# Widening a block's rows on ScalarE instead of VectorE, and scaling the routed rows ahead of the gelu

## What is computed

```python
logits = xt @ Wr + br
probs = softmax(logits)
top_p, top_idx = top_k(probs, 2)
weights = top_p / top_p.sum(axis=-1, keepdims=True)
xn = (xt - mu) * rsqrt(var + LN_EPS)
xe = xn[None, :, :] * ln_g[:, None, :] + ln_b[:, None, :]
h = gelu(einsum('end,edh->enh', xe, W1) + b1[:, None, :], approximate=False)
y = einsum('enh,ehd->end', h, W2) + b2[:, None, :]
out = (weights[:, :, None] * sel).sum(axis=1)
```

## Time and profile before

| | us |
|---|---|
| median of 3 runs | 3103.79 |
| lowest and highest | 3102.59, 3106.05 |
| the profiled execution | 3109.04 |
| its span in the trace | 3107.2 |
| blocks begin, about | 2237 into the span |
| blocks with tiles, two a step | about 2320 to 2771 |
| blocks alone | about 2771 to 3098 |

### The profile page before, as it was taken

The page is one execution under the profiler, slowest core; times in us unless marked ns, Lnnn a source line. Parts: engine busy times, 40 slices in busy tenths (PEclk is TensorE's granted clock), DMA queues, the critical chain, the costliest instruction groups (busy, mean ns, idle before and its releaser), DMA issues. The chain is left out here.

```text
span 3107.2 us, 76649 instructions
## 1 busy us (share of the span) xinstructions
PE 2657.0 (86%) x21213; PEld 1906.9 (61%) x21213; DVE 1716.7 (55%) x6061; ACT 1507.1 (49%) x4666; POOL 1972.3 (63%) x2053
## 2 busy tenths in 40 slices
PE   8898878878788878878888787885589999999998
PEld 6665445545454544545444444553479999999998
DVE  6466555555555555555555555556676556553222
ACT  5555444444444444444444454443466566554332
POOL 7277777777777777777777777775455455343222
PEclk9999988889898889888889898887599999999999
DMA  7688888888888888888888888886667677667664
GB/s 232 190 236 249 238 248 238 245 242 240 247 240 247 239 242 245 239 249 239 243 245 241 246 238 244 241 239 188 206 209 216 200 225 217 191 192 208 188 182 127
DMA packets 292076, 701.47 MB, mean 226 GB/s; under 512 B 44041, under 2 KB 139680, under 8 KB 291797
## 3 DMA queue, kind: packets, MB, share of 16 engines
q0 software_dynamic: 151888, 456.15, 52.2%
q1 hardware_dynamic: 140036, 243.55, 25.5%
HBM read 633.18 MB, written 66.36 MB: 225 GB/s over the span
## 5 line engine op out<-in xcount | busy, mean ns | idle before, releaser
L257 POOL DMA_INDIRECT e_kv<-d_kv,idx x1566 | 1498.6, 957 | 532.2 <-issue 510.5
L500 PE MATMUL psK<-consts,e_kv 128*128 128x128 f32 x3132 | 555.3, 305 | 295.9 <-DMA e_kv<-d_kv,idx 291.5
L500 PEld LDWEIGHTS psK<-consts,e_kv 128*128 128x128 f32 x3132 | 373.3, 152 | 430.0 <-issue 418.9
L397 DVE COPY e_kT<-psK 128x384 f32<-128x384 f32 x522 | 289.7, 555 | 323.9 <-PE psK L500 320.8
L1591 POOL DMA_INDIRECT out<-f_y,f_whose x105 | 166.9, 1590 | 473.2 <-DMA out<-f_y,f_whose 241.9
L1659 ACT ACTIVATE f_hT<-f_psH,f_b 128x128 f32<-128x128 f32 x840 | 237.0, 372 | 352.9 <-PE f_psH L2114 347.9
L2114 PE MATMUL f_psH<-f_xT,f_w 128*128 128x128 f32 x3360 | 400.1, 278 | 0.9 <-DVE f_xT L1957 0.9
L2114 PEld LDWEIGHTS f_psH<-f_xT,f_w 128*128 128x128 f32 x3360 | 391.7, 194 | 3.5 <-issue 1.3
L2127 PE MATMUL f_psY<-f_w,f_hT 128*128 x1680 | 381.8, 380 | 6.0 <-DVE f_yb L1967 4.1
L336 ACT COPY e_kT<-psK 128x384 f32<-128x384 f32 x522 | 249.9, 479 | 244.7 <-PE psK L500 227.3
L330 ACT COPY e_qb<-QT 64x32 f32 x1044 | 229.3, 220 | 279.2 <-issue 251.5
(11 more groups left out here) (309 smaller groups left out, 4013.3 us busy)
## 6 DMA issues: line engine op xcount, KB each, us to landing
f_w<-in_W SPq DMA_DIRECT2D x113, 1024.0 KB, 5.2
e_rows<-d_feat SPq DMA_DIRECT2D x174, 288.0 KB
e_kv<-d_kv,idx POOLq DMA_INDIRECT x1566
d_accs<-e_accs SPq DMA_DIRECT2D x87, 195.0 KB
f_xs<-d_xs SPq DMA_DIRECT2D x105, 132.5 KB, 4.9
d_kv<-p_kv SPq DMA_DIRECT2D x48, 256.0 KB, 2.1
p_x<-in_x SPq DMA_DIRECT2D x49, 128.0 KB, 2.9
n_v<-d_kv SPq DMA_DIRECT2D x49, 128.0 KB, 4.9
```

The lines of the kernel that those rows point to most:

```text
L257: pool.indirect_dma_start(out=kv[g.slot][:, t, :], out_offset=None, in_=kv_dram[:, :], in_offset=bass.IndirectOffsetOnAxis(ap=idx[g.slot][ ...
L397: dve.tensor_copy(kT[a.slot % 2][:, 0, j * GH:(j + 1) * GH], psK[:, 0, 0:GH]).then_inc(s_kTv, 1)
L500: mm = pe.transpose(psK[:, half, t * P:(t + 1) * P], kv[a.slot][:, third * TS + t, half * P:(half + 1) * P], ident)
```

## The change

`widen` leaves VectorE. ScalarE gets a function `widened`, laid at the head of a step for its first block, and for the second block behind the first one's gelu. It reads the expert's number into a register, and `bent` uses that same register, where it read its own before. Each of the two instructions is an activation of the function Identity, whose scale and bias are the expert's columns of `f_ln`. `sent` moves in steps with blocks from behind the first block's gelu to ahead of it.

```diff
-            def bent(g):
+            def widened(g):
                 if g == 0:
                     act.wait_ge(s_cv, 3)
+                act.wait_ge(s_T, g + 1)
+                e = act.value_load(rows[0:1, g:g + 1], min_val=0, max_val=NX - 1)
+                if g >= 2:
+                    act.wait_ge(s_h, (g - 1) * FC)
+                for a in range(DC):
+                    act.activation(xT[g % 2][:, a, :], psT[:, a * BK:(a + 1) * BK], ACT.Identity,
+                                   bias=ln[:, a, bass.ds(e + NX, 1)], scale=ln[:, a, bass.ds(e, 1)]).then_inc(s_xT, 1)
+                return e
+
+            def bent(g, e):
                 table(ACT.Gelu)
-                act.wait_ge(s_h, g * FC + FB)
-                e = act.value_load(rows[0:1, g:g + 1], min_val=0, max_val=NX - 1)
                 for f in range(FC):
...
                 if k is not None and not here:
                     gate(k)
+                expert = [widened(g) for g in here[0:1]]
                 if b is not None or k is not None:
                     table(ACT.Sqrt)
...
                 if not here:
                     sent(s)
+                if here:
+                    sent(s)
                 for u, g in enumerate(here):
-                    bent(g)
-                    if u == 0:
-                        if k is not None:
-                            gate(k)
-                        sent(s)
+                    if u:
+                        expert.append(widened(g))
+                    bent(g, expert[u])
+                    if u == 0 and k is not None:
+                        gate(k)
...
-            def widen(g):
-                dve.wait_ge(s_T, g + 1)
-                e = dve.value_load(rows[0:1, g:g + 1], min_val=0, max_val=NX - 1)
-                if g >= 2:
-                    dve.wait_ge(s_h, (g - 1) * FC)
-                for a in range(DC):
-                    dve.tensor_scalar(xT[g % 2][:, a, :], psT[:, a * BK:(a + 1) * BK],
-                                      ln[:, a, bass.ds(e, 1)], ln[:, a, bass.ds(e + NX, 1)],
-                                      ALU.mult, ALU.add).then_inc(s_xT, 1)
...
                 if here:
                     for _ in first:
                         pass
-                    widen(here[0])
...
-                    for g in here[1:]:
-                        widen(g)
```

## The result

The changed kernel takes 3128.24 us (median of 4 runs, 3127.48 to 3131.43), the kernel before 3104.53 in the same comparison. The ratio is 1.0075, 95% interval 1.0063 to 1.0086: slower by 24 us, where 32 were forecast.

The account below looks back on a forecast made before the run. PE's list was taken to bound the kernel, with ScalarE's `n_h` ending last in 21 steps. Terms +29.8 + 5 + 1.6 - 4 = +32, laid on the median 3103.79, gave 3136 us, range 3112 to 3153.

Parts of the forecast that it names:

- What bounds it: From 2320 on PE's list sets the time; in 21 two-block steps ScalarE's piece from last gelu to `n_h` ends last.
- Widening ahead of `n_h`: At the head of two-block steps, `n_h` 1.15 us later, 21 steps paying it in full; +29.8 us together.
- The pair: The widening's two Identity activations on ScalarE, put at 0.86 us, bounded by 0.64 and 1.08.
- the register load: ScalarE's read of the expert's number between last gelu and table load, taken as 0.39 us, bounds 0 and 0.82.
- rival B: Same mechanism, smaller: load hidden under the gelus, pair near 0.64, routed rows free; +11, 3115 us; chance 24%.
- Gelus 0.1 us earlier: Gelus of the block before no longer wait for a register load of their own; 0.1 us gained at most.
- Second block and blocks alone: There PE's second product covers the widening, with 1.0 us of cover; cost nothing.
- Routed rows: Laid ahead of the first block's gelu, they delay it in 8 steps with three tiles; +5 us (0 to 10).
- First block: Its widening, needing the transposes, stands before `n_h`, so the first product starts later, once; +1.6 us.
- VectorE relieved: Each block frees 1.12 us on VectorE, which shortens steps of one block and later waits around GpSimd; -4 us.
- Table loads and the other lists: Table loads keep number and kind, and PE's, GpSimd's and SP's lists stay the same; nothing.
- Rival C: Faster: VectorE makes steps long, so taking 1.12 us per block from it counts; 3091 us; chance 9%.

Follow-up runs that it names:

- k4_before_nh_first: The kernel before with `n_h` ahead of `n_xn` in steps with blocks, nothing else; 3100.38 us, ratio 0.9990.
- k1_sent_back: The changed kernel with the scaling of the routed rows put back behind the first block's gelu; 3120.34 us, ratio 1.0054 to the kernel before.
- k10_second_only: The kernel before with only the second block of each step widened on ScalarE; ratio 1.0004, on a slower chip.
- k3_nh_first: The changed kernel with routed rows put back and step heads ordered `n_h`, widening, `n_xn`; 3095.20 us, ratio 0.9976 to the kernel before.
- k7_again: The changed kernel with superfluous widening work at VectorE's old places, second run, on a slower chip; ratio 1.0055 to the kernel before.

## Why the prediction was right, and where it was off

- **What bounds it.** Right. PE's list sets the pace, and in 21 steps `n_h` already ended last; `k4_before_nh_first` took exactly the 0.31 us of the earlier trace rows off a plain step. The constant 0.73 us between `n_h` and PE's transposes holds in every kernel where `n_h` is the last to come.
- **Widening ahead of `n_h`, +29.8.** Mechanism right, size too large. Forecast 1.15 us per step, measured 0.75 in a plain step, in 27 steps 20 us. Measured in one piece, from the `n_h` of step 23 to that of step 50, `k1_sent_back` took 17.3 us more than the kernel before (467.1 against 449.8), in which the 2.4 us of waits for VectorE are already given back. The pair was near: 0.81 for 0.86; that it is 0.08 slower than VectorE's 0.73 is worth 2 us of the 20. The term that failed is the register load, taken as 0.39 from the earlier trace rows. On ScalarE it costs 0: its sequencer begins to read at 2328.92, when two of the gelus (2329.04 and 2329.29) have yet to begin. VectorE's sequencer, in the earlier trace rows, begins only after the predecessor has:

```profile
L1953 DVEq TENSOR_LOAD <-rows x1: 313/313/313, 2386.5 to 2386.5; - x1
```

The predecessor starts at 2386.52 and runs 0.42 us; from the load's start to the widening's it is 0.8. My explanation of the difference: the gelus don't wait for one another, so the sequencer hands them on and goes ahead; in VectorE's chain each operation waits for the one before, and the sequencer with it. Shown are the two starts, the hidden first load and the 0.55 us of the second; no run changed the predecessor alone. The prediction had both bounds and chose the wrong one, and with it rival B's argument was the better one on this point: with the load at 0 its own sum would have been +22, near the 24 measured.
- **Gelus 0.1 us earlier, -0.1 per step.** Nothing came of it. They start earlier, but in two groups of four, and the second still waits for the end of the first product, 0.64 us in the row above.
- **Second block and blocks alone, 0.** Right: `k10_second_only`'s plain step is 16.55, and PE is busy 318.1 of 319 us in the last window.
- **Routed rows, +5 (0 to 10).** Right in kind and within its range, toward the upper end: 6.5 us by the times, 7.1 and 10.2 by the stage. The raw sum of 10.5 was reduced for waits given back. PE waited 8.2 for `f_hT`, and 2.4 of waits for `f_yb` and `f_y` vanished.
- **First block, +1.6.** The first product starts 118.4 us into the stage instead of 116.3: +2.1 in this pair of traces, +1.3 in that of `k1_sent_back`.
- **VectorE relieved, -4.** The sum is about right by luck, the place wrong. From the first product to step 23, where it was forecast, only 1.0 us came back; PE still waited 3.45 us for `n_h` where it had waited 4.21, and the product behind that pause was still slow, 6.38 us, at a granted clock of 0.66 from 2280 to 2290. Behind step 50, where nothing was forecast, 3.0 came back.
- **Table loads and the other lists, 0.** Nothing in the traces speaks against it.
- **Rival C and the rule of balance.** VectorE at 272 of 451 us was not what PE waited for, so relieving it moved a few microseconds. The Trainium skill (Perfetto Trace Analysis, Optimizing Scalar/DVE Operations) suggests such a move where VectorE is saturated. This VectorE wasn't, and the trace agrees so far as the move brought little; no run here has a saturated one.

The signs came as forecast, each somewhat smaller: from the last gelu's end to `n_h` 2.75 us (3.2 was forecast), PE's wait there 0.87 (1.4), and the mean of the 23 steps 17.8 ((2741.68 - 2332.42) / 23; 18.0). The forecast of +32 was off by 8: the load was put too high by 10.5, the routed rows too low by a few.

The stage grew by 25.6 us: 20 (`n_h`) + 7 (routed rows, less the waits given back) + 2.1 (first block) - 1.0 - 3.0 = 25. How the 27.5 us of the 27 steps divide depends on the side from which one comes: taken out of the changed kernel the routed rows are 10.2 of them and leave 17.3 for the widening; added to the kernel before they are 6.0 and leave 21.5.

## What to carry to other kernels

Before work is moved to the less busy engine, look at what stands behind the place in its list into which it goes: two activations in front of the one on which PE waits cost 20 us, and the same two behind it nothing. That `k3_nh_first` is even faster than the kernel before comes in good part from `n_h` having passed `n_xn` too, which `k4_before_nh_first` does with no work moved at all. A pause of a tenth of a microsecond that the profile calls "issue" may be a dependence; a distance that is the same in every step tells. In these traces a register load was free behind gelus, with 0.75 us of them left to run, cost 0.55 us as a second load behind the first, and left a hole of 0.39 us behind a chain in which each operation waits for the one before.

## What the runs showed that was not expected

ScalarE hides one register load under the last gelus, and charges 0.55 us for the second. Swapping two neighbours in ScalarE's list, `n_xn` and `n_h`, and moving no work, makes the kernel before faster by 3.7 us (7.2 in the stage).

The two chips of the last eight runs took 3811 and 3802 us for the kernel before, 700 more than the first ones. The trace of `k7_again` on one of them and that of the kernel before move the same bytes, 701.5 MB; the mean rate is 183 against 226 GB/s because the span is longer:

```profile
DMA packets 292078, 701.50 MB, mean 183 GB/s; under 512 B 44040, under 2 KB 139679, under 8 KB 291796
```

The stage starts 2751.6 us into the span instead of 2123.3, so most of the 700 lies ahead of what was changed. Within it, steps in which batches are scattered take 21 to 26 us instead of the changed kernel's 18 to 19, while plain steps agree to 0.01 us with those of the first chips: 17.30 for the widening as changed, 16.24 with `n_h` first. Where an experiment's time is drowned in such a difference, a distance inside the step still measures. Why these chips are slower isn't known, and a ratio from them can't be set beside one from the first chips without doubt.
